# Attention over 4096 context tokens: value projections move to two score banks, and their fifth passes run as paired 64-row products

## What is computed

```
q, k, v = x_norm @ Wq', ctx_768 @ Wk', ctx_768 @ Wv'        # W' = W + down @ up * alpha / rank
s = einsum('bhid,bhjd->bhij', q, k) * 64 ** -0.5
o = einsum('bhij,bhjd->bhid', softmax(s), v)
out = (o + o_ipa) @ Wo + bo + lora(o + o_ipa)               # o_ipa: attention to the last 4 tokens
```

## Time and profile before

| | |
|---|---|
| median of three runs | 2002.29 us |
| the profiled execution, first to last instruction | 2003.2 us |
| its mean granted TensorE clock | 0.947 |
| TensorE busy | 1821.4 us, 91% |
| ScalarE, VectorE, GpSimd busy | 51%, 50%, 33% |
| unit 0's keys, maxima and first values | from 93 to 134 us |
| double steps of the 16 units | from about 138 to 1130 us |

### The profile page before, as it was taken

The page is one execution under the profiler, slowest core; times in us unless marked ns, Lnnn a source line. Parts: engine busy times, 40 slices in busy tenths (PEclk is TensorE's granted clock), DMA queues, the critical chain, the costliest instruction groups (busy, mean ns, idle before and its releaser), DMA issues. The chain is left out here.

```text
span 2003.2 us, 32608 instructions
## 1 busy us (share of the span) xinstructions
PE 1821.4 (91%) x13272; PEld 1277.3 (64%) x13272; DVE 994.6 (50%) x1502; ACT 1026.5 (51%) x1395; POOL 668.9 (33%) x331
## 2 busy tenths in 40 slices
PE   6889999999999999999999776779999999666999
PEld 2567777777667777777766544448445744344887
DVE  3566666675665756566561244337001500374665
ACT  1245555555545555555541231216898799434443
POOL 2007566575555756556583213003000100110000
PEclk9899999999999999999997888789999999877999
DMA  5450000000301200000030200024652555200220
GB/s 194 129 191 7 6 11 6 17 6 7 95 7 51 98 6 17 1 17 6 1 81 4 63 0 0 19 63 111 136 101 51 127 96 96 85 1 32 87 95 21
DMA packets 80804, 107.38 MB, mean 54 GB/s; under 512 B 22088, under 2 KB 63792, under 8 KB 76560
## 3 DMA queue, kind: packets, MB, share of 16 engines
q1 hardware_dynamic: 78160, 103.75, 19.4%
q10 hardware_dynamic: 2496, 1.54, 0.3%
HBM read 62.77 MB, written 21.50 MB: 42 GB/s over the span
## 5 line engine op out<-in xcount | busy, mean ns | idle before, releaser
L773 POOL TENSOR_TENSOR sums<-sums,probs 128x1024 f32<-128x1024 f32 x224 | 532.6, 2378 | 335.8 <-ACT probs L808 319.2
L872 DVE TENSOR_REDUCE part_max<-psum_banks 128x2 f32<-128x1024 f32 (+1 forms) x256 | 312.8, 1225 | 129.7 <-PE psum_banks L1046 127.7
L808 ACT ACTIVATE probs<-psum_banks 128x1024 f32<-128x1024 f32 x240 | 233.6, 1022 | 115.0 <-PE psum_banks L1093 114.5
L863 DVE TENSOR_TENSOR keys<-psum_banks,keys 64x512 fp32r<-64x512 f32 x256 | 176.3, 689 | 186.6 <-ACT keys L786 182.3
L2487 ACT ACTIVATE probs<-psum_banks,k_inv_norm 128x1024 f32<-128x1024 f32 x256 | 258.0, 1267 | 2.1 <-PE psum_banks L2502 2.1
L1107 PE MATMUL psum_banks<-probs,values 128*64 128x256 f32 x2048 | 251.0, 388 | 0.0
L786 ACT ACTIVATE keys<-psum_banks 64x512 fp32r<-64x512 f32 x256 | 151.8, 593 | 173.7 <-PE psum_banks L1021 170.1
L1107 PEld LDWEIGHTS psum_banks<-probs,values 128*64 128x64 f32 x2048 | 136.6, 137 | 87.2 <-issue 30.9
L791 ACT ACTIVATE values<-psum_banks 128x512 f32<-128x512 f32 x128 | 76.6, 599 | 200.6 <-PE psum_banks L1033 200.6
L2514 PE MATMUL psum_banks<-probs,values 128*32 128x256 f32 x2048 | 166.0, 397 | 3.0 <-ACT probs L2487 3.0
L1075 PEld LDWEIGHTS psum_banks<-q_hi,keys 128*128 128x128 f32 x1024 | 141.6, 192 | 13.1 <-issue 1.8
(11 more groups left out here) (430 smaller groups left out, 2865.0 us busy)
## 6 DMA issues: line engine op xcount, KB each, us to landing
k_pairs<-keys SPq DMA_DIRECT2D x192, 128.0 KB, 4.1
c_parts<-ctx_parts SPq DMA_DIRECT2D x48, 256.0 KB, 3.7
wk_pair<-wkv_parts SPq DMA_DIRECT2D x16, 256.0 KB, 2.9
wv_quad<-wkv_parts SPq DMA_DIRECT2D x8, 512.0 KB, 3.8
ctx_parts<-cA_hi SPq DMA_DIRECT2D x2, 2048.0 KB, 11.4
ctx_parts<-cA_lo SPq DMA_DIRECT2D x2, 2048.0 KB, 12.9
ctx_parts<-cB SPq DMA_DIRECT2D x2, 2048.0 KB, 17.6
w_gate_up<-in_L_ffn_gate_proj_w SPq DMA_DIRECT2D x8, 512.0 KB, 3.8
```

What stands on the lines that cost most here:

```text
L773: pool.tensor_tensor(sums[:, :, :, :], probs[:, 0, :, :, :] if step == 1 else sums[:, :, :, :], probs[:, step % SLOTS, :, :, :], ALU.add). ...
L808: act.activation(probs[:, step % SLOTS, :, :, :], scores, ACT.Exp, scale=SCALE0).then_inc(p_ready, 1)
L863: dve.tensor_tensor(keys[rows(1 - h), m % 2, h, columns_of(c)], psum[rows(h), bank, :], keys[rows(h), m % 2, h, columns_of(c)].bitcast(F32 ...
L872: dve.tensor_reduce(part_max[:, :, i, c], psum[:, bank:bank + 2, 0:width], AX, ALU.max).then_inc(m_read, 1)
```

## The change

The values of a chunk of 512 tokens become one piece. It has four token tiles; the even tiles go to one bank and the odd tiles to the next. In the double steps these are banks 4 and 5, the banks of the even score step; ahead of the loop they are 6 and 7. Its TensorE part waits for the even step's exponentials, and the next double step's `begin_scores` waits until ScalarE has taken the values out. Two pieces of ScalarE work stay two, one for each bank.

The fifth pass leaves its low-times-low half out. For the odd tiles of `cB`, VectorE writes the low part to rows 0 to 63 and the high part stays in rows 64 to 127, so an even tile has its high part below and an odd tile above. The fifth pass of an even tile then reads rows 0 to 63 and that of an odd tile rows 64 to 127, each a product of 64 rows by 256 columns, and the two go to different banks. The four fifth passes of a chunk are issued first. The VectorE instruction that writes the low part of `cB` becomes two of half the columns, eight times at the start and eight times in unit 6. Ahead of the loop the two maxima pairs of a chunk are now issued one after the other, with the values behind them.

```
+def own_half(chunk, parity):
+    rows = slice(CB, P) if parity == 0 else slice(0, CB)
+    return chunk[rows, :].rearrange("p (g two n) -> p g two n", two=2, n=P)[:, :, parity, :]
...
-            behind[(2 * quad - 1) * TWOS + c] += [("values", quad, 2 * c), ("values", quad, 2 * c + 1)]
+            behind[values_at(quad, c)] += [("values", quad, c)]
...
-        out += [("max", 0, c, 0), ("values", 0, 2 * c), ("max", 0, c, 1), ("values", 0, 2 * c + 1)]
+        out += [("max", 0, c, 0), ("max", 0, c, 1), ("values", 0, c)]
...
             if piece[0] == "values":
-                return piece[2] % 2 + (6 if alone else 0)
+                return 6 if alone else 4
...
+                        if not alone:
+                            pe.wait_ge(p_ready, 2 * values_at(quad, c) + 3)
+                        elif c >= 1:
+                            pe.wait_ge(v_kept, 2 * c)
...
                         for j in range(2):
-                            tile = slice((2 * step + j) * P, (2 * step + j + 1) * P)
-                            for k, (part, operand) in enumerate(PASSES):
-                                last = pe.matmul(psum[:, bank, j * QW:(j + 1) * QW], operand[:, tile], wv_q[:, part, :],
-                                                 start=k == 0, stop=k == len(PASSES) - 1)
-                        last.then_inc(v_done, 1)
+                            for parity in range(2):
+                                pe.matmul(psum[:, bank + parity, j * QW:(j + 1) * QW], cB[rows(parity), tile(j, parity)],
+                                          wv_q[rows(parity), 3, :], start=j == 0, stop=False)
+                        for parity in range(2):
+                            for j in range(2):
+                                for k, (part, operand) in enumerate(PASSES[:4]):
+                                    last = pe.matmul(psum[:, bank + parity, j * QW:(j + 1) * QW], operand[:, tile(j, parity)],
+                                                     wv_q[:, part, :], start=False, stop=j == 1 and k == 3)
+                            last.then_inc(v_done, 1)
...
 def begin_scores(m, step):
...
+                    before = m * TWOS + step // 2 - 2
+                    if step % 2 == 0 and before >= TWOS and before // TWOS % 2 == 1 and before < (UNITS - 2) * TWOS:
+                        pe.wait_ge(v_kept, (before // TWOS + 1) // 2 * STEPS + before % TWOS * 2 + 2)
```

More of the change, by code:

```diff
@@ L456, in low @@
                                       ALU.subtract).then_inc(lo_ready, 1)
-                    dve.tensor_tensor(cB[CB:P, columns_of(i)], psum[CB:P, 2 * (i % 2) + 1, :],
-                                      cB[CB:P, columns_of(i)].bitcast(F32), ALU.subtract).then_inc(lo_ready, 1)
+                    for parity in range(2):
+                        part = low_half(cB, i, parity)
+                        last = dve.tensor_tensor(part, own_half(psum[:, 2 * (i % 2) + 1, :], parity), part.bitcast(F32),
+                                                 ALU.subtract)
+                    last.then_inc(lo_ready, 1)
                 dve.wait_ge(tok_turned, 1)
@@ L597, in low_queries_at, with values_at @@
     return (m - 1) * TWOS + (3 + h if m % 2 == 0 else -1)
+def values_at(quad, c):
+    return (2 * quad - 1) * TWOS + c
 def pieces_of_double_steps():
@@ L640, in l0_attention @@
     for g in range(FIRST, END):
-        in_bank0 += ahead[g] + [("spread", m) for m in range(1, UNITS) if g == spread_at(m)] + behind[g][:1]
-        in_bank1 += top[g] + behind[g][1:]
+        in_bank0 += ahead[g] + [("spread", m) for m in range(1, UNITS) if g == spread_at(m)]
+        in_bank0 += [piece for piece in behind[g] if piece[0] == "turn_a"]
+        in_bank1 += top[g] + [piece for piece in behind[g] if piece[0] == "turn_b"]
     previous = {**dict(zip(in_bank0[1:], in_bank0)), **dict(zip(in_bank1[1:], in_bank1))}
@@ L788, in prepare @@
                     if kind == "values":
[L789 to L792, removed]
+                        _, quad, c = piece
+                        kept = values[:, 4 * c:4 * c + 4, :].rearrange("p (t two) n -> p two t n", two=2)
+                        for parity in range(2):
+                            act.wait_ge(v_done, quad * STEPS + 2 * c + parity + 1)
+                            act.activation(kept[:, parity, :, :], psum[:, bank + parity, :].rearrange("p (t n) -> p t n", t=2),
+                                           ACT.Copy).then_inc(v_kept, 1)
                     if kind in ("turn_a", "turn_b"):
@@ L880, in prepare @@
                         dve.wait_ge(ctx_hi, 2 * c + 2)
-                        dve.tensor_tensor(cB[CB:P, columns_of(c)], psum[CB:P, bank, :], cB[CB:P, columns_of(c)].bitcast(F32),
-                                          ALU.subtract).then_inc(ctx_lo, 1)
+                        for parity in range(2):
+                            part = low_half(cB, c, parity)
+                            last = dve.tensor_tensor(part, own_half(psum[:, bank, :], parity), part.bitcast(F32), ALU.subtract)
+                        last.then_inc(ctx_lo, 1)
                 def maxima(m):
@@ L1009, in prepare @@
                     kind, bank = piece[0], bank_of(piece, alone)
-                    if not alone:
+                    if not alone and kind != "values":
                         wait_for_bank(piece)
@@ L1024, in prepare @@
                     if kind == "values":
[L1025 to L1028, removed]
+                        _, quad, c = piece
+                        if not alone:
+                            pe.wait_ge(p_ready, 2 * values_at(quad, c) + 3)
+                        elif c >= 1:
+                            pe.wait_ge(v_kept, 2 * c)
+                        if c == 0:
                             pe.wait_ge(wv_in, (quad + 1) * 16)
+                        tile = lambda j, parity: slice((4 * c + 2 * j + parity) * P, (4 * c + 2 * j + parity + 1) * P)
                         for j in range(2):
-                            tile = slice((2 * step + j) * P, (2 * step + j + 1) * P)
-                            for k, (part, operand) in enumerate(PASSES):
-                                last = pe.matmul(psum[:, bank, j * QW:(j + 1) * QW], operand[:, tile], wv_q[:, part, :],
-                                                 start=k == 0, stop=k == len(PASSES) - 1)
-                        last.then_inc(v_done, 1)
+                            for parity in range(2):
+                                pe.matmul(psum[:, bank + parity, j * QW:(j + 1) * QW], cB[rows(parity), tile(j, parity)],
+                                          wv_q[rows(parity), 3, :], start=j == 0, stop=False)
+                        for parity in range(2):
+                            for j in range(2):
[3 more added lines that the diff above has]
+                            last.then_inc(v_done, 1)
                     if kind == "max":
@@ L1099, in weigh @@
                     if n % 2 == 0:
-                        pe.wait_ge(v_kept, n // 2 * STEPS + step + 1)
+                        pe.wait_ge(v_kept, n // 2 * STEPS + step // 2 * 2 + 2)
                     if step == 0 and n >= 1:
```

4 lines of the change are left out of this document (2 added, 2 removed).

## The result

| | before | changed |
|---|---|---|
| median, us | 2004.01 (4 runs, 2000.6 to 2006.02) | 1976.72 (4 runs, 1974.54 to 1982.63) |
| ratio, 95% interval | | 0.9863 [0.9845, 0.9881] |
| medians of a second set of runs | 2003.62 (14 runs) | 1974.65 (5 runs), ratio 0.9866 [0.9846, 0.9886] |
| heavy double step, the first six of a unit's eight | 8.54 to 8.58 | 8.11 |
| the last two of the eight | 8.98 to 9.07 | 8.52 to 8.55 |

The kernel became 27.3 us faster; the forecast was 28.7 us, and 1976.7 lies in the range of 1969 to 1984.

The account below looks back on a forecast made before the run. TensorE's own list was taken to bound the kernel. Gains of 25.2, 0.6 and 3.8 us less 0.9 for VectorE made 28.7 us, so 1973.6 us measured; range 1969 to 1984 us.

Parts of the forecast that it names:

- What bounds: 155 to 1060 us: TensorE busy 893 of 905 us at clock 1.00, so shortening its list shortens the kernel.
- The fifth passes: Heavy steps, behind the maxima pair: paired 64-row products cost 0.23 us and replace four full products worth 0.47 us.
- Rival 1: Fifth passes pay for a change of shape or don't run side by side: 1985 to 1987 us, chance 0.05.
- The wait in the middle: Among a heavy step's values, TensorE waits 0.21 us for VectorE to read the maxima's bank; the change removes it.
- the shift's share: In seven heavy steps values also waited for the shift to leave bank 0; half of 1.2 us counted, 0.6 us.
- The new wait: Next scores wait for the copy of the second values bank: margin 0.09 to 0.20 us, cost taken as 0.
- Rival 2: The scores' wait for the values' copy is met slightly late, 0.1 to 0.2 us a step: 1979 to 1985 us, chance 0.09.
- Rival 3: In begin_scores, the wait for late copies takes more than the gain: 1996 to 2013 us, slower; chance 0.04.
- Rival 4: GpSimd or VectorE sets the pace of the shorter steps and takes the gain back: 1985 us or more, chance 0.02.
- Ahead of the loop: Chunks before the loop shorten from 4.75 to 4.2 us, saving 3.8 us over seven; bounds 1 and 5.8.
- VectorE's halves: Splitting cB's low-part instruction adds 0.18 us each; five of eight at the start counted, 0.9 us; unit 6, 0.
- The signs of being wrong: Scores' load over 1.16 us behind keys', 0.3 us gap between maxima and fifth passes, or clock below 1, 155 to 1030 us.

Follow-up runs that it names:

- e7: Changed kernel with the odd tiles' fifth passes also reading rows 0 to 63, so both tiles share rows: 1983.97 us, ratio 0.991.
- e3: Changed kernel with the paired fifth passes between the even tiles' full products and the odd tiles': 1998.14 us, ratio 0.9973.
- e1: Changed kernel with all five passes as full 128-row products and cB's old layout; new banks, waits and order kept: 1986.59 us, ratio 0.9916.
- e2: Changed kernel with ScalarE copying both banks of values out only after all products of the piece are done: 1993.13 us, ratio 0.9944.
- e4: Changed kernel with the four fifth passes issued even, even, odd, odd instead of even, odd, even, odd: 1972.03 us, ratio 0.9856.
- e8: Changed kernel run again without an edit, on the chip of a later set of runs: 1974.65 us, ratio 0.9866.
- e5: Changed kernel with values back in banks 0 and 1, paired fifth passes between the full products after the maxima wait: 2009.18 us, ratio 1.0034.
- e9: Changed kernel with a score step's six 64-row products issued head by head, in all 128 double steps: 1970.87 us, ratio 0.9836.

## Why the prediction was right, step by step

**What bounds.** TensorE's list does: the earlier trace rows had clock 1.00 and a TensorE with hardly any idle time, and each term taken off the list came back in full (25.7 us out of the 56, 25.8 forecast).

**The fifth passes.** Forecast 0.23 us behind the maxima, measured 0.67 - 0.42 = 0.25. Their form could be priced from `finish_scores`, and e7 shows that the price hangs on the rows differing. Rival 1 (a change of shape, or no side by side) would have shown as 8.3 us; it fell. e7 has the price of its second half, 0.24 us; for the first half e3 has 0.39 us for a passage in and one out, some 0.2 each, as forecast.

**The wait in the middle.** Forecast 12.4 with the shift's share, measured 12.5 (e1).

**The new wait.** Taken as 0; the scores' load stands 1.06 us behind the keys', forecast 1.05. Rival 2 fell, with the margin confirmed by e2. Rival 3's place was right: copies made late do delay the scores, but by 0.30 us a step and not 0.40, still a gain over before (0.9944). Rival 4 fell too: the shorter steps came out at the sum of TensorE's own terms, and GpSimd's 4.9 us of work in each fits well below.

**Ahead of the loop.** Forecast 4.2 us a chunk and 3.8 us in all. Measured 4.23, and 3.35 us in the first pair of executions (40.86 - 37.51); 3.48 in e4, whose half clock lasted as long as before's and whose chunks have the same work:

```profile
93.21:130.59 37.38, 36.49 (x232) 29.02 (x233) 30.96 (x36) 20.11 (x35) 0.25 (x2) 0.93 0.84 289
```

Against e8 it would be 4.2 us (40.86 - 36.66), but 0.7 us of that is the clock. So the term was over-sized by 0.3 to 0.5 us. The wait for VectorE's maxima that was worked out beforehand is there, in every second chunk, 0.2 us each.

**VectorE's halves.** This term was over-sized. The two halves take 2 x 0.42 us as expected:

```profile
L470 DVE TENSOR_TENSOR cB<-psum_banks,cB x16: 415/422/428, 63.3 to 93.3; 64x256 fp32r<-64x256 f32 x16
```

But from the first transposed tokens to the first keys it is 33.48 us before and 33.58 in e1, which has whole instructions, against 33.64 to 33.88 in nine executions with halves: 0.1 to 0.4 us, not 0.9. The four shortest of the nine had the full clock for longer in this stretch; the other five, at about e1's clock, are 0.2 to 0.3 us above e1. Of the five instructions that I counted, the time of one or two lies on the path; which, no run here shows. For the eight in unit 6, forecast at 0, the stretch between the two groups of heavy steps is 67.97 us before and 68.41 after, so it cost at most 0.4 us.

**The sum.** 25.7 + 3.4 - 0.3 is 28.8 us, 28.7 forecast. That it is so near is in part luck: the term ahead of the loop was up to 0.5 us too large, and the halves were priced 0.6 us too high, which took it back. The medians differ by 27.3 and 29.0 us. What is left lies in parts that the change does not touch: the stretch behind the last `weigh` was 3.6 us longer in one execution of the changed kernel, and the one behind the last values takes 116 to 125 us, by its clock. The single pairs of executions show how little one total says: 2003.2 - 1980.9 = 22.3 us for the first, 2003.2 - 1968.3 = 34.9 us with e8.

**The signs of being wrong.** The scores' load and the start of the fifth passes stayed within theirs. The granted clock did fall below 1 between 155 and 1030 us, but no more than before: 0.98 from 505 to 573 us, where it had been 0.97 from 518 to 586. It says nothing against the mechanism.

## What to carry to other kernels

When one engine's list sets the time, price a change by the starts in its timeline: each product by a neighbour of the same shape, and each passage by a neighbouring passage. Five such terms gave 28.7 us of 27 to 29. Here products of half the rows gained only where others of their kind already stood (13.2 us), not in the middle of full ones (e3, e5); so look first for what keeps them from that place, here a bank that another engine still read. Before a bank is handed to a new user, add up when its last reader is seen done against the latest load that delays nothing; here that left 0.17 us, and a second copy that ended 0.48 us later used it up. When single executions are compared, cut them at the same events and look at the granted clock of each stretch first: 0.7 us of clock looked like a gain ahead of the loop.

## What was unexpected of the hardware

TensorE did not keep its products strictly in the order in which the code issues them: those on rows 64 to 127 overtook waiting ones on rows 0 to 63 at no cost (e4, four products, 8.11 us; e9, six, 5.99 us), while the same four on one set of rows took 0.23 us more (e7). The Trainium skill ("TensorE: Matmul & The Clock Gate", Part 3) has matmuls start and end strictly in program order; the runs differ. In order, e9 would have lost 0.78 - 0.46 = 0.32 us in every score step, worked out from rows of this case, and taken some 2050 us; it took 1970.87. The records don't name rows, so the overtaking is read from the durations and from the grouping, not seen product by product. And two of ScalarE's copies of 128 x 512 out of PSUM back to back took 1.08 us, where one alone takes 0.60.
